# Gated rows' statistics moved into attention, with another order between attention and scatters

## The reference

```python
def layernorm(x): return (x - mean(x)) / sqrt(var(x) + 1e-5)
# 1: attention of 4 heads of 32, over xn = layernorm(x), masked by adj
scores = clip(q @ k.T / sqrt(32), -10, 10); scores[adj == 0] = -10
out = (softmax(scores) @ v) @ Wo.T + bo + xn
x = x + layernorm(out) * gamma + beta
# 2: the two best of 8 experts per row
xf = layernorm(x)
probs = softmax(xf @ gate_w + gate_b); best two of 8 -> weights we
x = x + sum over the two of we * (gelu(xf @ W1[e] + b1[e]) @ W2[e] + b2[e])
```

## Time and profile before

| what | us |
|---|---|
| median of the runs (lowest, highest) | 821.14 (819.8, 823.19) |
| the profiled execution's own time | 818.33 |
| its span, first to last instruction | 816.2 |
| busy: PE, DVE, ACT, POOL | 670.1, 690.6, 561.5, 558.7 |
| mean granted TensorE clock | 0.895 of full |

### The profile page before, as it was taken

The page is one execution under the profiler, slowest core; times in us unless marked ns, Lnnn a source line. Parts: engine busy times, 40 slices in busy tenths (PEclk is TensorE's granted clock), DMA queues, the critical chain, the costliest instruction groups (busy, mean ns, idle before and its releaser), DMA issues.

```text
span 816.2 us, 20212 instructions
## 1 busy us (share of the span) xinstructions
PE 670.1 (82%) x6427; PEld 389.0 (48%) x6427; DVE 690.6 (85%) x1753; ACT 561.5 (69%) x1091; POOL 558.7 (68%) x571
## 2 busy tenths in 40 slices
PE   4698399999999999999999973846610699999994
PEld 1433134434334334344342322735510599999994
DVE  4989989999799999999999998786670499899993
ACT  4697288996998989989988754525300477777772
POOL 1210808798798998989989999778777055555554
PEclk9699899999999999999999997555655699999998
DMA  8926105536226145162261104001111222232210
GB/s 277 248 82 157 55 20 156 154 99 173 94 93 159 60 124 152 55 176 81 98 155 66 53 1 104 1 28 31 54 50 53 53 66 71 81 83 75 63 49 2
DMA packets 58850, 74.53 MB, mean 91 GB/s; under 512 B 8172, under 2 KB 33609, under 8 KB 58746
## 3 DMA queue, kind: packets, MB, share of 16 engines
q1 hardware_dynamic: 41114, 41.59, 16.9%
q10 hardware_dynamic: 12672, 23.07, 10.9%
q0 software_dynamic: 4960, 8.58, 3.3%
HBM read 52.38 MB, written 22.59 MB: 92 GB/s over the span
## 4 chain that ended last, share of the span: by engine, by line
PE 45%; DVE 22%; ACT 10%; issue 9%; POOL 8%; DMA 4%; SPq 1%; ACTq 1%; POOLq 0%; DVEq 0%
PE score_ps L1534 7%; PE sum_ps L1548 7%; PE side_ps L1564 6%; DVE prob_ring L1015 5%; POOL rows_dram L630 4%; DVE w L1015 3%; DVE prob_ring L1026 3%; ACT xn L706 2%; DVE rspread L1037 2%; PE score_ps L1492 2%; PE score_ps L1494 2%; PE score_ps L1493 2%; PE sum_ps L1778 2%; PE sum_ps L1776 2%; PE sum_ps L1774 2%
## 5 line engine op out<-in xcount | busy, mean ns | idle before, releaser
L1534 PE MATMUL score_ps<-stack_mem 128*128 128x512 f16 x512 | 140.4, 389 | 27.0 <-DVE prob_ring L1015 22.1
L1015 DVE SCALAR_TENSOR_TENSOR w<-score_ps,limit 128x1024 f32<-128x1024 f32 x128 | 150.2, 1217 | 12.8 <-PE score_ps L1534 12.7
L784 ACT ACTIVATE prob_ring<-prob_ring 128x1024 f32<-128x1024 f32 x128 | 133.2, 1054 | 34.3 <-DVE prob_ring L1015 29.0
L1015 DVE SCALAR_TENSOR_TENSOR prob_ring<-score_ps,limit 128x1024 f32<-128x1024 f32 x128 | 149.5, 1210 | 6.9 <-PE score_ps L1534 6.3
L568 POOL TENSOR_TENSOR ctx_sb<-ctx_sb,rspread 128x512 f32<-128x512 f32 x108 | 139.1, 1288 | 19.4 <-POOL ctx_acc L573 9.6
L637 POOL DMA_INDIRECT out_x<-xn,limit x91 | 90.6, 995 | 85.8 <-DVE xn L1389 70.6
L784 ACT ACTIVATE w<-w 128x1024 f32<-128x1024 f32 x128 | 134.0, 1053 | 19.0 <-DVE w L1015 13.0
L573 POOL TENSOR_TENSOR ctx_acc<-ctx_acc,ctx_sb 128x512 f32<-128x512 f32 x93 | 119.4, 1284 | 7.3
L909 ACT ACTIVATE xn<-score_ps,vec 128x128 f32<-128x128 f32 x364 | 99.1, 383 | 11.4 <-PE score_ps L1494 10.4
L1534 PEld LDWEIGHTS score_ps<-stack_mem 128*128 128x128 f16 x512 | 37.7, 98 | 126.2 <-issue 53.0
L630 POOL DMA_INDIRECT rows_dram<-x,limit x64 | 64.7, 1012 | 19.9 <-issue 18.8
(11 more groups left out here) (238 smaller groups left out, 1592.8 us busy)
## 6 DMA issues: line engine op xcount, KB each, us to landing
rspread<-rinv_dram SPq DMA_DIRECT2D x70, 256.0 KB
stack_mem<-qk_dram ACTq DMA_DIRECT2D x56, 256.0 KB, 5.0
ctx_sb<-rows_dram SPq DMA_DIRECT2D x91, 66.5 KB, 2.0
qk_dram<-qk_hi ACTq DMA_DIRECT2D x16, 256.0 KB, 2.8
qk_dram<-qk_lo ACTq DMA_DIRECT2D x16, 256.0 KB, 5.5
x<-in_adj SPq DMA_DIRECT2D x4, 512.0 KB, 7.5
ctx_sb<-in_adj SPq DMA_DIRECT2D x4, 512.0 KB, 9.9
stack_mem<-qk_dram SPq DMA_DIRECT2D x16, 128.0 KB, 3.3
```

The source lines that it names most:

```text
L784: act.activation(prob_at(s, u), prob_at(s, u), ACT.Exp, scale=1.0 / SCORE).then_inc(exp_done, 1)
L1015: dve.scalar_tensor_tensor(out=prob_at(s, u), in0=score_ps[:, 2 * u:2 * u + 2, :], scalar=-LIMIT * SCORE, in1=limit[:, k:k + 1, half * HAL ...
L1534: ins = pe.matmul(score_ps[:, h, :], kstack[:, par, h, k * P:k * P + P], qstack[:, par, h, half * HALF:half * HALF + HALF], start=True, st ...
```

## The change

1. The statistics of batches 0 to 4 are made inside attention: gate_stats in two halves at steps 8 and 13 of batch b + 2 on DVE, gate_moments at step 0 of batch b + 3, and root3 at step 3 of batch b + 3 on POOL. Mean and variance go straight into the row's columns; stats3 and moments3 fall away. Batches 5 to 7 stay behind attention.
2. SHUFFLED goes from 3 to 2: the third chunk's spread row of each of the 14 groups of eight comes by DMA instead of by two shuffles.
3. x2 of batch 0 is made by ACT in steps 14 and 15 of the last batch, and waits for the scores of batch 6 alone.
4. post_final of batch 7 moves from POOL to DVE (last_final), and last_contexts is cut into last_products and last_sums, which stand apart.
5. ACT, DVE, PE and POOL have another order between attention and scatters.

Constants, and POOL (its root3 now reads and writes the row's columns in place):

```diff
-    SHUFFLED = 3
+    SHUFFLED = 2
...
-    RSTD, SHIFT, SHARES, TOKEN = D, D + 1, D + 2, D + 4
+    SHIFT, RSTD, SHARES, TOKEN = D, D + 1, D + 2, D + 4
...
+                    if s == 3 and b >= 3:
+                        root3(b - 3)
...
             normalise(LAST, STEPS - 7)
-            root3(0)
             normalise(LAST, STEPS - 6)
             normalise(LAST, STEPS - 5)
-            root3(1)
             post_final(LAST - 1, 1)
             post_root(2 * LAST)
-            root3(2)
-            post_final(LAST, 0)
-            root3(3)
             scatter(range(0, T))
+            root3(5)
+            root3(6)
+            scatter(range(T, 3 * T))
             post_root(2 * LAST + 1)
-            post_final(LAST, 1)
-            root3(4)
-            scatter(range(T, T + 4))
-            root3(5)
-            scatter(range(T + 4, 2 * T))
-            root3(6)
+            scatter(range(3 * T, 4 * T))
             root3(7)
-            scatter(range(2 * T, TILES))
+            scatter(range(4 * T, TILES))
```

ACT (x2 now takes the tiles, and its activations are the same):

```diff
+                if tiles[0] == 0:
+                    act.wait_ge(shift3_ready, b + 1)
+                    act.wait_ge(qk_done, 2 * STEPS * (NB if b else LAST))
...
+                    if s in (14, 15) and last:
+                        x2(0, range((s - 14) * TH, (s - 14) * TH + TH))
```

DVE:

```diff
+            def gate_stats(b, half):
+
+                dve.wait_ge(x1_ready, 2 * b + 3)
+                wait(dve, moments3_ready, b - 1)
+                for t in range(half * TH, half * TH + TH):
+                    ins = dve.bn_stats(stats[:, b % 2 * T + t, :], x1_tiles(b)[:, t, :])
+                if half == 1:
+                    ins.then_inc(stats3_done, 1)
+
+            def gate_moments(b):
+
+                dve.wait_ge(stats3_done, b + 1)
+                for t in range(T):
+                    ins = dve.bn_aggr(x1_rows(b)[:, t, SHIFT:SHIFT + 2], stats[:, b % 2 * T + t, :])
+                ins.then_inc(moments3_ready, 1)
...
+                    if s in (8, 13) and b >= 2 and not last:
+                        gate_stats(b - 2, s // 13)
+                    if s == 0 and b >= 3:
+                        gate_moments(b - 3)
...
+            def last_final(half):
+
+                n = 2 * LAST + half
+                dve.wait_ge(x_beta_ready, NB)
+                dve.wait_ge(y_ready, n + 1)
+                dve.wait_ge(x1_ready, n + 1)
+                dve.tensor_tensor(res[:, half, :, :], res[:, half, :, :], rows_bc[:, 1:2, :].to_broadcast([P, TH, P]),
+                                  ALU.mult).then_inc(y_scaled, 1)
+                dve.wait_ge(y_scaled, n + 1)
+                x1_half = x1_tiles(LAST)[:, half * TH:half * TH + TH, :]
+                dve.tensor_tensor(x1_half, res[:, half, :, :], x1_half, ALU.add).then_inc(x1_ready, 1)
```

PE:

```diff
-            pe.wait_ge(res_ready, 2 * LAST)
-            wo(2 * LAST)
...
+            pe.wait_ge(clip_done, 2 * STEPS * NB)
+            turn_x2(0)
+            turn_x2(1)
+            pe.wait_ge(res_ready, 2 * LAST)
+            wo(2 * LAST)
+            gate(0)
+            gate(1)
+            gates(1)
             pe.wait_ge(ctx_copied, STEPS * NB)
-            pe.wait_ge(clip_done, 2 * STEPS * NB)
-            gates(0)
+            prefix(0)
+            gates(2)
             pe.wait_ge(res_ready, 2 * LAST + 1)
             wo(2 * LAST + 1)
-            gates(1)
-            prefix(0)
-            gates(2)
             gates(3)
             prefix(1)
             gates(4)
+            prefix(2)
             gates(5)
-            prefix(2)
             gates(6)
+            prefix(3)
             gates(7)
-            prefix(3)
             prefix(4)
```

More of the change, by code:

```diff
@@ L608, in root3 @@
                 rstd, shift = x1_rows(b)[:, :, RSTD], x1_rows(b)[:, :, SHIFT]
-                own = slice(T * b, T * b + T)
                 pool.wait_ge(moments3_ready, b + 1)
-                pool.tensor_scalar(rstd, moments3[:, own, 1], EPS, 1.0, ALU.add, ALU.mult).then_inc(root3_step, 1)
-                pool.tensor_scalar(shift, moments3[:, own, 0], -1.0, 1.0, ALU.mult, ALU.mult)
+                pool.tensor_scalar(rstd, rstd, EPS, 1.0, ALU.add, ALU.mult).then_inc(root3_step, 1)
+                pool.tensor_scalar(shift, shift, -1.0, 1.0, ALU.mult, ALU.mult)
                 pool.wait_ge(root3_step, 2 * b + 1)
@@ L785, in exp, with x2 @@
                                ACT.Exp, scale=1.0 / SCORE).then_inc(exp_done, 1)
+            def x2(b, tiles):
+                if tiles[0] == 0:
+                    act.wait_ge(shift3_ready, b + 1)
+                    act.wait_ge(qk_done, 2 * STEPS * (NB if b else LAST))
+                for t in tiles:
+                    ins = act.activation(x2_mem[:, T * b + t, :], x1_tiles(b)[:, t, :], ACT.Identity,
+                                         bias=x1_rows(b)[:, t, SHIFT:SHIFT + 1], scale=x1_rows(b)[:, t, RSTD:RSTD + 1])
+                    if t % TH == TH - 1:
+                        ins.then_inc(x2_ready, 1)
             def body(b, par=None):
@@ L821, in _ @@
                 ctx_copy(LAST, s)
[L822 to L834, removed]
             def x2T_copy(c):
@@ L860, in turned @@
                 x2T_copy(2 * b + 1)
-            x2(0)
             turned(0)
-            x2(1)
+            post_y(2 * LAST - 1, range(TH))
+            x2(1, range(T))
             gate_exponent(0)
+            x2(2, range(T))
             turned(1)
+            turned(2)
+            x2(3, range(T))
             post_y(2 * LAST, range(TH))
-            x2(2)
-            turned(2)
-            x2(3)
             gate_exponent(1)
             turned(3)
-            post_y(2 * LAST + 1, range(TH))
[L874 to L880, removed]
+            x2(4, range(T))
+            turned(4)
+            gate_exponent(2)
+            x2(5, range(T))
+            turned(5)
+            x2(6, range(T))
+            turned(6)
+            post_y(2 * LAST + 1, range(TH))
             gate_exponent(3)
@@ L883, in _ @@
             w1_high(1)
-            x2(7)
+            x2(7, range(T))
             turned(7)
@@ L1091, in _, with stats_of @@
             copy_consts()
+            def gate_stats(b, half):
[10 more added lines that the diff above has]
+                ins.then_inc(moments3_ready, 1)
+            def stats_of(b):
+                gate_stats(b, 0)
+                gate_stats(b, 1)
+                gate_moments(b)
             def body(b, par=None):
@@ L1131, in _ @@
             batches(body)
[L1132 to L1142, removed]
             def per_tile(v, n):
@@ L1391, in combine, with tail_slots, last_products, last_sums @@
                                          op1=ALU.add).then_inc(rows_ready, 1)
-            def last_contexts():
-                g, first = STEPS * LAST, STEPS - TAIL
-                slots = [ctx_sb[:, (g + s) % RING, :] for s in range(first, STEPS)]
+            def tail_slots():
+                return [ctx_sb[:, (STEPS * LAST + s) % RING, :] for s in range(STEPS - TAIL, STEPS)]
+            def last_products():
+                slots = tail_slots()
                 dve.wait_ge(ctx_copied, STEPS * NB)
-                for s in range(first, STEPS):
-                    dve.wait_ge(rspread_ready, shuffles_by(g + s))
-                    dve.tensor_tensor(slots[s - first], slots[s - first], rspread[:, s % SPREADS, :], ALU.mult).then_inc(tail_step, 1)
+                for s in range(STEPS - TAIL, STEPS):
+                    j = s - (STEPS - TAIL)
+                    dve.wait_ge(rspread_ready, shuffles_by(STEPS * LAST + s))
+                    dve.tensor_tensor(slots[j], slots[j], rspread[:, s % SPREADS, :], ALU.mult).then_inc(tail_step, 1)
+            def last_sums():
+                slots = tail_slots()
                 for j in range(1, TAIL):
@@ L1404, in last_contexts @@
                 dve.wait_ge(tail_step, 2 * TAIL - 1)
[L1405 removed]
+                dve.wait_ge(chunk_added, STEPS * LAST + STEPS - TAIL)
                 dve.wait_ge(wo_done, 2 * LAST)
                 dve.tensor_tensor(ctxT[:, 1, :], ctx_acc[:], slots[0], ALU.add).then_inc(chunk_added, TAIL)
+            def last_final(half):
[8 more added lines that the diff above has]
+                dve.tensor_tensor(x1_half, res[:, half, :, :], x1_half, ALU.add).then_inc(x1_ready, 1)
             spread(LAST, STEPS - TAIL - 2)
@@ L1427, in _ @@
             gate_logits(0)
-            stats_of(2)
+            stats_of(5)
             gate_choice(0)
-            stats_of(3)
+            last_products()
             gate_slots(0)
+            last_sums()
             gate_logits(1)
+            stats_of(6)
+            gate_choice(1)
+            last_final(0)
+            gate_slots(1)
+            gate_logits(2)
             post_res(LAST, 1)
@@ L1435, in _ @@
             post_moments(2 * LAST + 1)
[L1436 to L1440, removed]
+            gate_choice(2)
+            gate_slots(2)
+            last_final(1)
             stats_of(7)
-            gate_logits(2)
```

(4 more changed lines are left out.)

5 lines of the change are left out of this document (removed).

## The result

The kernel after takes 816.62 us in the median (813.86 to 819.46), the kernel before beside it 821.87 (817.15 to 825.58): the ratio is 0.9948 [0.9933, 0.9963]. It is 5.2 us faster by the medians and 4.3 (3.0 to 5.5) by the ratio, about half of the 9.9 that were forecast. The profiled execution took 815.88 us, its span is 814.1.

What follows compares the result with a forecast made beforehand. POOL was taken as the bound, in the last batch and through the scatters behind attention. Attention 4.1 us late, first scatter at 525.0, last ending at 622.2 instead of 632.1: 9.9 us off, 811 us by the median, range 803 to 818.

Steps and rivals of the forecast that it cites:

- part 2: DVE in attention: statistics cost 2.3 us per batch, saved shuffles give time back; net +0.3 us per batch 2 to 6.
- 14 more of 256 KB ... the price is nothing: Added spread-row loads in attention: issued 12.4 us before POOL needs them, so cost nothing unless other loads come late.
- Rival D: Six spread-row loads per group come late for POOL, three us more per batch over five batches: 826 us; chance 0.03.
- It doesn't add to the 4.1: DVE's net in batches 2 to 6 adds nothing to POOL's 4.1 us: in batch 7 POOL is later than DVE.
- Part 1, the roots: POOL in attention: 2.4 us per root, all of it in batch 7, 1.7 lag from batches 3 to 6; 4.1 us late.
- POOL's idle time would be near nothing: Sign in attention: moved roots use up POOL's waits for DVE's moments (1.5 us) and ACT's post_y (0.8) in batches 3 to 6.
- Parts 3 and 4: Behind attention: first scatter at 525.0 instead of 532.01; scatters with 3.5 us of waiting end at 622.2 instead of 632.14.
- A: Roots are free in attention, POOL's waits hide them all, batch 7 included: 807 us; chance 0.18.
- E: The change doesn't take hold, first scatter stays at 532, held by something other than x2(0) and roots: 818 us; chance 0.08.
- B: The gate chain, not POOL, sets the scatters, with 4 to 5 us more waiting: 815 us; chance 0.15.
- C: POOL becomes attention's bound, each root costs 3.8 us, attention ends 19.0 us late: 826 us; chance 0.04.
- batches longer than 54.5 us: Sign that the forecast is wrong: attention's batches, 54.0 us before, grow past 54.5 us, pointing to C or Rival D.

Runs made afterwards that it cites:

- e4: Kernel after with begin_rows' 29 DMAs moved from the third group to behind the last group: 808.45 us, ratio 0.9856 to the kernel before.
- e1: Kernel after with SHUFFLED back at 3, everything else of the change kept: 809.43 us, ratio 0.9865 to the kernel before.
- e2: Kernel before with SHUFFLED at 2 and no other part of the change: 828.03 us, ratio 1.0088 to the kernel before.
- g1: Kernel after, begin_rows late, two shuffles in groups inverted at step 10, three in those at step 2: 802.18 us, ratio 0.9775 to before.
- g2: Kernel after, begin_rows late, three shuffles in groups inverted at step 10, two in those at step 2: 810.25 us, ratio 0.9863 to before.
- f1: Kernel after with SHUFFLED at 3 and begin_rows late: 823.59 us, ratio 0.9788 to before; again on a third chip 806.97 us, 0.9839.
- f4: Kernel before with begin_rows late and nothing else: 839.31 us, ratio 0.997 to the kernel before, on a slower chip.
- f2: Kernel after with SHUFFLED at 3 and the roots of batches 1 to 4 behind attention: 830.85 us, ratio 0.9868 to before, slower chip.
- e3: Kernel after with stack loads at steps 9 and 12 and the second store at step 9: 824.25 us, ratio 1.0042 to the kernel before.
- g3: Kernel after, begin_rows late, two shuffles in groups inverted at step 10, four in those at step 2: 800.97 us, ratio 0.9762 to before.
- f3: Kernel after with only the second stack's loads at step 11 instead of 10: 830.01 us, ratio 0.9871 to before, on a slower chip.

## Why the prediction was half right

**The sum.** The forecast was 811 us and 9.9 us of gain, with faster as the likeliest; the direction, and the gain behind attention, came as worked out. Compared with the forecast of the last scatter's end, 622.2, the 629.76 are made up of: ACT's resumption at 498.17 instead of 488.5, +9.7; from there to the first scatter 36.1 instead of 36.5, -0.4; the scatters 95.5 instead of 97.2, -1.7. These are +7.6, all of the error on the profiled execution. The 9.7 are the delay at the start of batch 7. By the medians the error is 5.6 us, since the profiled execution of after stands 0.7 us below its median, that of before 2.8 below the median used.

**The step that failed** is in part 2: "14 more of 256 KB ... the price is nothing". I had set the issue of the loads against the moment at which POOL needs them, 12.4 us, and in batches 3 to 6 that held. In batch 2, where begin_rows' 29 DMAs come on top, even that failed: POOL waited for loads in after, and in no stretch of before.

```profile
POOL ctx_sb L566 <- DMA rspread<-rinv_dram: 5.6, 4, 2.3
```

In e4, with as many loads and begin_rows elsewhere, it waits for none, and batches 3 to 6 are as slow as in after (222.4 us against 220.9). But a load has two prices, its own landing and what it does to transfers beside it. ACT's stores and stack loads lay in the same steps, their landing was waited for in ACT's list, and no row of mine asked about them. e1, e2 and the pair g1 and g2 show it. Rival D had the right resource, but named POOL as the victim, and so had a chance of 0.03. Of the 9.7 us the third shuffle gives back 4.4 (e1); with begin_rows moved too it is 8.3 (f1 again: 433.8). The two overlap, since begin_rows delays the loads of batch 2 into the store and the sixth load comes on top. begin_rows stood there in before as well, and moving it was no part of the change.

**Part 2, the statistics.** Forecast +0.3 us a batch, bounds -0.7 and +0.9. With the loads out of the way it is +0.8 with three shuffles (f1 against f4) and about +0.1 with two in one group (g1: 54.1 against 54.0). So the estimate of the DVE account was fair; what the shuffles give back can be had only where the load that takes their place is free. "It doesn't add to the 4.1" was the second step that failed: the delay of batches 2 to 6 was put at nothing, but a late start of batch 7 adds to the lag within it. With begin_rows late and three shuffles, so without the harm of the loads, this late start is 3.3 us (f1 against f4).

**Part 1, the roots.** The root in attention takes 2.35 us as taken, with the row of its power among them:

```profile
346.03 0.21 POOL L608 TENSOR_SCALAR x<-x 128x8 f32<-128x8 f32 x1
...
346.49 1.66 POOL L611 TENSOR_TENSOR x<-x,neg_half 128x8 f32<-128x8 f32 x1
348.22 0.21 POOL L613 TENSOR_TENSOR x<-x 128x8 f32<-128x8 f32 x1
```

In batch 7 ctxT of step 7 ends 69.4 us after the start, before 65.3: 4.1 late, as forecast. It is POOL that takes this time. The stretches from the first clip of batch 7 to the end of that ctxT, before and after:

```profile
432.40:497.65 65.25, 54.76 (x537) 19.60 (x535) 61.78 (x137) 45.29 (x60) 60.25 (x53) 1.00 0.10 33
```

```profile
442.08:511.44 69.36, 55.13 (x520) 19.39 (x522) 57.51 (x124) 48.73 (x70) 64.20 (x59) 0.95 0.11 38
```

POOL is busy 60.25 and 64.20 us in them and idle 5.0 and 5.2. How far behind POOL is when the batch starts can be read from its post_root(11): it starts 1.25 us after the first clip in before (433.65) and 3.09 after it in after (445.17). So 1.8 of the 4.1 us are work left over from batch 6, and 2.3 are the root. The same two terms fit every kernel. Length less this lag is 64.0 us in the four kernels without a root in batch 7 (before, e2, f2, f4) and 66.2 to 66.3 in the ten with one, while the length itself goes from 63.6 (e3) to 69.9 (e4). So the 2.4 for the root of batch 7 held. The 1.7 for the lag came true by luck: it was to come from the roots of batches 3 to 6, but e1 and f2, with and without most of these roots, have the same lag, 2.3 us, and f1 has 0.7. Two shuffles and no roots at all make it 3.1 (e2). The 13.8 us by which attention ends late are 9.7, 2.3 and 1.8.

The forecast that POOL's idle time would be near nothing was wrong. What POOL waited for in batches 3 to 6 of after:

```profile
POOL res L593 <- ACT res L708: 5.0, 4, 1.9
```

Its wait for DVE's moments (5.3 us in before) is gone, but it now waits 5.0 us for ACT's post_y (2.0 in before), as ACT is late itself. I had taken the releasers of before as fixed.

**Parts 3 and 4** held: without the shift of 9.7 the first scatter would stand at 524.6, forecast 525.0. The wait before the ninth was 1.50 us instead of 3.5; 1.1 of the difference are last_sums, whose three additions took 2.13 us (533.27) instead of 3.25. The two roots took 5.3 us (5.2 taken). A scatter beside w1_low took 1.96 us at 595.72, before 1.47.

**The rivals.** A and E aren't what happened, B (POOL waits over 8 us between scatters) neither. C is refuted by the root's 2.35 us and by f2. Of my signs, "batches longer than 54.5 us" was the one that rightly pointed away from the forecast.

**Not settled:** how the loads hold up a store while most of the DMA engines' time is free (last section), and why the ratio of one kernel, f1, differs by 0.5% between two chips. In two executions of one kernel (f1) batch 7 starts 0.9 us apart, so smaller differences of positions weren't read.

## What to carry to other kernels

A DMA that is added for a consumer which waits for nothing isn't free yet: list the other transfers in flight in those steps and who waits for each, above all an engine that computes and also waits, in its own order, for a store to land before it issues a load. Between DVE work and a transfer the choice can be made group by group: the same change of seven groups was worth +4.8 us or -3.3 us, by the steps in which its loads ran. A wait put down to "issue" in front of a compute instruction is to be read with the DMA-issuing rows ahead of it in the timeline.

## What the hardware showed that was not expected

A store of 256 KB on ACT's queue landed in 2.0 to 13.2 us in before, after and g3 (13.6 in e2, 14.3 in f3), by what SyncE's queue carried at the time. The median of the ten stores of qk_lo from 150 to 445 us was 5.6 us in before, 6.4 in after and 3.8 in g3. The longest of all stores from 100 to 445 us were 7.7, 13.2 and 6.3 us. The DMA engines were busy for 40% of the batch in the mean, and that mean hid the delay. So does the share of a shorter stretch: while the loads run alone (350 to 357 us of after) it is 0.26 at 102 GB/s, and in the last 6.0 us before the late store landed, with loads and store both in flight, it was 0.23:

```profile
200.00:206.00 6.00, 2.92 (x30) 0.99 (x28) 5.71 (x12) 0.00 (x0) 4.47 (x7) 1.00 0.23 83
```

So the engines as a whole weren't full; which of them the store waited for isn't shown. The Trainium skill ("DMA: Bandwidth & Descriptors", Queues, rings and completion order) says that SyncE's and ACT's queues use the same 16 DMA engines, and that each engine takes turns between the queues that have work, a packet at a time. The traces agree in that a store is slower while the other queue has work: 13.20 us beside the loads of batch 2, and for the first qk_lo stores of batches 1 to 6 2.3 to 2.5 us in g3, with four loads in that group, against 6.4 to 7.3 in after, with six.
